# A three-stage transformer kernel: setup work moved between engines, the end of self-attention reordered, feed-forward weights turned one group at a time

## The reference, cut to what matters

```python
x = x + xattn(ctx_1024, ctx_1024, layernorm(x), lens, lens, ...)   # 32 batches, 64 queries, 1601 keys, 16 heads of 16
x = x + attn(layernorm(x), ...)          # causal self-attention with position bias, projection, a layernorm of its own
x = x + ffn(layernorm(x), ...)           # quantised feed-forward, inner size 768

# ffn:
x = act_qdq(x); up = act_qdq(x @ dq(w_up).T); gate = act_qdq(x @ dq(w_gate).T)
gate = act_qdq(gate * fixed_qdq(sigmoid(gate)))
return act_qdq(gate * up) @ dq(w_down).T
```

## Time and profile before

| | |
|---|---|
| median of 3 executions | 1581.92 us (1581.59 to 1583.39) |
| profiled execution | 1582.63 us, of which the span of instructions is 1580.8 us |
| PE busy | 1389.4 us (88%) |
| DVE busy | 1061.8 us (67%) |
| ACT busy | 881.5 us (56%) |
| POOL busy | 789.2 us (50%) |
| cross-attention, setup and batch -1 | 0 to 92.7 us |
| cross-attention, batches 0 to 31 | to about 1215 us |
| self-attention | to 1392.3 us |
| feed-forward | to 1580.8 us |

### The profile page before, as it was taken

One profiled execution on the slowest core, in us unless ns is written; L12 is line 12 of the kernel. 1 busy time (PEld: TensorE's weight loads), 2 busy tenths in 40 slices (PEclk: granted clock), 3 DMA queues, 4 the chain that ended last, 5 costly groups with the idle time before them and its releaser, 6 DMA issues. The chain is left out here.

```text
span 1580.8 us, 55267 instructions
## 1 busy us (share of the span) xinstructions
PE 1389.4 (88%) x24351; PEld 989.7 (63%) x24351; DVE 1061.8 (67%) x1681; ACT 881.5 (56%) x1195; POOL 789.2 (50%) x560
## 2 busy tenths in 40 slices
PE   4679999999999999999999999999997687459408
PEld 2457777777777777777777777777775355324107
DVE  7756666666666666666666666666664867785984
ACT  1445655665656565665556565656565565425742
POOL 4566555555655555555555555555530798420000
PEclk9899999999999999999999999999999898769859
DMA  4564444544444444444444444444421421010001
GB/s 150 145 137 137 107 107 110 128 120 120 117 127 132 107 107 116 121 124 122 114 136 121 107 107 120 124 124 114 117 65 53 131 54 27 1 41 0 1 0 54
DMA packets 90495, 155.97 MB, mean 99 GB/s; under 512 B 16704, under 2 KB 55496, under 8 KB 90256
## 3 DMA queue, kind: packets, MB, share of 16 engines
q1 hardware_dynamic: 88256, 150.92, 36.6%
q10 hardware_dynamic: 2000, 1.51, 0.4%
HBM read 60.95 MB, written 2.20 MB: 40 GB/s over the span
## 5 line engine op out<-in xcount | busy, mean ns | idle before, releaser
L645 DVE TENSOR_REDUCE MXP<-W_PS 128x1 f32<-128x512 f32 x768 | 510.7, 688 | 339.8 <-PE W_PS L456 338.7
L540 ACT ACTIVATE PR<-S_PS 128x1024 f32<-128x1024 f32 (+1 forms) x416 | 409.0, 1030 | 144.8 <-PE S_PS L404 142.8
L350 POOL TENSOR_TENSOR K_HI<-K,MCOL 128x512 f16<-128x512 f32 (+1 forms) x224 | 215.2, 961 | 282.8 <-ACT K L548 282.8
L356 POOL TENSOR_TENSOR CTX_LO<-CTX,CTX_HI 128x3202 f16<-128x3202 f32 x32 | 194.1, 6067 | 190.9 <-DVE CTX_HI L623 190.9
L456 PE MATMUL W_PS<-STK,QS 105*128 105x512 f16 (+1 forms) x1024 | 279.9, 336 | 10.1 <-POOL STK L377 6.1
L548 ACT ACTIVATE K<-W_PS,BK 128x512 f32<-128x512 f32 (+1 forms) x256 | 148.3, 593 | 175.9 <-PE W_PS L430 157.1
L404 PE MATMUL S_PS<-QS,STK 105*128 105x128 f16 (+1 forms) x3328 | 238.9, 220 | 4.2 <-ACT PR L540 2.9
L352 POOL TENSOR_TENSOR K_LO<-K,K_HI 128x512 f16<-128x512 f32 (+1 forms) x224 | 232.0, 1036 | 17.6
L404 PEld LDWEIGHTS S_PS<-QS,STK 105*128 105x128 f16 (+1 forms) x3328 | 210.4, 99 | 48.2 <-ACT PR L540 3.8
L439 PE MATMUL W_PS<-WV_HI,CTX_HI 128*128 128x256 f16 (+1 forms) x832 | 228.0, 274 | 2.8 <-ACT K L548 2.6
L439 PE MATMUL W_PS<-WV_HI,CTX_LO 128*128 128x256 f16 (+1 forms) x832 | 227.4, 273 | 0.0
(11 more groups left out here) (243 smaller groups left out, 1593.5 us busy)
## 6 DMA issues: line engine op xcount, KB each, us to landing
CTX<-in_ctx_t SPq DMA_DIRECT2D x64, 800.5 KB, 5.8
STK<-K_HI SPq DMA_DIRECT2D x256, 128.0 KB, 2.5
STK<-K_HI SPq DMA_DIRECT2D x256, 72.1 KB, 2.1
STK<-K_LO SPq DMA_DIRECT2D x128, 128.0 KB, 2.6
STK<-K_LO SPq DMA_DIRECT2D x128, 72.1 KB, 2.1
QSTK<-STK SPq DMA_DIRECT2D x12, 192.0 KB
SQS<-QK_HI SPq DMA_DIRECT2D x32, 64.0 KB, 2.2
X<-in_x SPq DMA_DIRECT2D x1, 1536.0 KB, 16.3
```

What stands on the lines that cost most here:

```text
L350: pool.tensor_tensor(K_HI[:, m, lo:hi], k32, zero, ALU.add).then_inc(k_hi, 1)
L356: pool.tensor_tensor(CTX_LO[:, u, :, :], CTX[:, :, :], CTX_HI[:, u, :, :], ALU.subtract).then_inc(ctx_lo, 1)
L540: nc.scalar.activation(PR[0:m, (NT * b + i) % PR_RING, :], S_PS[par][0:m, :], ACT.Exp).then_inc(p_sb, 1)
L645: dve.tensor_reduce(MXP[:, j, at:at + 1], bank[:, :], AX.X, ALU.max).then_inc(mx_done, 1)
```

## The change

It has three parts.

1. **Setup of cross-attention.** The high parts of the weights, of batch 0's context and of query chunk 0 are made by ACT; DVE makes the low parts, batch 0's `CTX_LO` among them, in two halves. For batches 0 and 1 ACT makes `K_HI` from the PSUM bank beside `K32`, and POOL only `K_LO`. The loads are issued in another order. ACT issues 6 of the 12 transfers of batch 0's first half stack (`SK`). The late layernorm root (`SQ`), rows (`RW`) and mask (`QM`) become steps of `FIRST`, whose order changes. The ones of `STK[1]` are copied from `STK[0]` by a DMA. `QSTK`'s memset moves ahead of batch 0 on POOL. PE runs 28 matmuls whose result nobody reads.
2. **End of self-attention.** `centred`, `normal_again`, the group products and `maximum(0)` are placed differently; the transposes `XT 0` move behind the pipeline.
3. **Feed-forward.** The weights are turned one group ahead of each of gate chunks 12 to 21; the first eight gate and up chunks are taken in another order; the first gate integer tensor is made by DVE, and ACT makes four up tensors first and then alternates.

```diff
+START = [("K", 0), ("QH", 0), ("K", 1), ("K", 2), ("K", 3), ("K", 4), ("K", 5), ("K", 6)]
 FIRST = [
...
+    ("V", 0), ("SK", 2), ("SK", 3), ("SQ", 1), ("V", 1), ("RW", 1), ("QM", 1), ("V", 2), ("V", 3), ("TN", 1),
+    ("CH", 0), ("RW", 2), ("V", 4), ("QS", 0), ("MX", 0), ("MX", 1), ("QY", 1), ("MX", 2), ("MX", 3), ("TN", 2),
+    ("RW", 3), ("MX", 4), ("MX", 5), ("V", 5), ("MX", 6), ("MX", 7), ("QY", 2), ("MX", 8), ("MX", 9), ("TN", 3),
+    ("MX", 10), ("MX", 11), ("V", 6), ("MX", 12), ("MX", 13), ("QY", 3), ("MX", 14), ("MX", 15), ("K", 0), ("MX", 16),
+    ("MX", 17), ("K", 1), ("MX", 18), ("MX", 19), ("K", 2), ("MX", 20), ("MX", 21), ("K", 3), ("MX", 22), ("MX", 23),
+    ("K", 4), ("MX", 24), ("MX", 25), ("MT", 0), ("K", 5), ("K", 6),
 ]
+EARLY_K = 2
...
+    def stack_rows(eng, u, c, lo, hi, done):
+        rows = slice(32 * c, 32 * c + 32)
+        for q, part in enumerate((K_HI, K_LO, K_HI)):
+            eng.dma_start(STK[u][32 * q:32 * q + 32, c::4, lo:hi], part[rows, :, lo:hi]).then_inc(done[c], 16)
...
         sp.wait_ge(q_rest, 16 * 13)
+        sp.dma_start(STK_MEM[1][ROW_M:ROW_MASK, :], STK_MEM[0][ROW_M:ROW_MASK, :]).then_inc(stk_m, 16)
...
         def ctx_low(n, u):
-            pool.wait_ge(ctx_hi, n + 1)
+            pool.wait_ge(ctx_hi, n + 2)
+            if n == 1:
+                pool.wait_ge(qs_ready, 2)
...
+        pool.wait_ge(k_lo, 2 * PER["K"])
+        pool.memset(QSTK[ROW_M:ROW_MASK, :, CH:ROWS].bitcast(F32), 0.0).then_inc(q_zero, 1)
...
-        pool.memset(STK_MEM[1][ROW_M:ROW_MASK, :].bitcast(F32), ones).then_inc(constant, 1)
...
+        pe.wait_ge(constant, 1)
+        idle(18)
+        pe.wait_ge(in_cst, 16 * 4)
         turn(0)
+        idle(10)
         query(0)
...
+                        for s, m in enumerate(range(ms.start, ms.stop)):
+                            last = nc.scalar.activation(K_HI[:, m, lo:hi], bank[:, s * LAST:s * LAST + hi - lo], ACT.Identity,
+                                                        bias=BK[:, m:m + 1], scale=1 / W_SCALE)
+                        last.then_inc(k_hi, 1)
...
+                elif kind == "SK":
+                    act.wait_ge(k_lo, 4)
+                    stack_rows(act, 0, i, 0, HALF, stk_a)
...
-ENDING = [("XT", 1, 0), ("XT", 1, 1), ("XT", 2, 0), ("XT", 2, 1), ("XT", 3, 0), ("XT", 3, 1)]
+ENDING = [("XT", 0, 0), ("XT", 0, 1), ("XT", 1, 0), ("XT", 1, 1), ("XT", 2, 0), ("XT", 2, 1), ("XT", 3, 0), ("XT", 3, 1)]
-WEIGHTED = {13: (0, 4), 14: (4, 8), 17: (8, 13)}
+WEIGHTED = {13: [(0, 4)], 14: [(4, 8)], 17: [(8, 10), (10, 13)]}
...
+            if s == 17:
+                act.wait_ge(sm["chain"], 2 * CHAIN)
+                centred(range(8, 10))
...
-            if s == 16:
-                act.wait_ge(sm["chain"], 2 * CHAIN)
-                centred(range(8, 13))
-                normal_again(range(0, 4))
             if s == 17:
-                normal_again(range(4, 8))
+                centred(range(10, 13))
+                normal_again(range(0, 8))
...
             if s == 18:
-                maximum(0)
                 add_weighted(2, 8, 13)
         dve.wait_ge(sm["y_stat"], 16 + 13)
         scale_rows(2)
+        maximum(0)
         add_rows(range(*GROUPS[2]))
...
-TURN = {8: 0, 16: 1}
+TURN = {12: (0, 0), 13: (0, 1), 14: (0, 2), 15: (0, 3),
+        16: (1, 0), 17: (1, 1), 18: (1, 2), 19: (1, 3), 20: (1, 4), 21: (1, 5)}
+UP_EARLY = 4
...
+    def place(i):
+        return (i % 2, i // 2) if i < 8 else (i // 4, i % 4)
...
+        for f in range(UP_EARLY):
+            up_integer(f)
         act.wait_ge(sm["sc"], 4 * SSTEPS)
-        for f in range(FT):
+        for f in range(1, FT):
             nc.scalar.activation(GI[:, f, :], G[:, f, :], ACT.Copy, scale=INV[:, 3:4]).then_inc(sm["g2i"], 1)
+            if UP_EARLY + f - 1 < FT:
+                up_integer(UP_EARLY + f - 1)
...
+        dve.tensor_scalar(GI[:, 0, :], G[:, 0, :], INV[:, 3:4], None, ALU.mult).then_inc(sm["giv"], 1)
```

More of the change, by code:

```diff
@@ L278, in stack @@
             lo, hi = (0, HALF) if half == 0 else (HALF, LK)
-            done = stk_a if half == 0 else stk_b
             if half == 0:
                 need(sp, s_ps, NT * (n - 1))
+                if n == 0:
+                    sp.wait_ge(mask_out, 16)
             sp.wait_ge(k_lo, PER["K"] * n + (4 if half == 0 else 7))
             if half == 0:
-                sp.dma_start(STK[u][ROW_MASK:ROW_MASK + 1, :, :],
-                             dram["kmask"][bass.ds(n, 1), :].rearrange("a (o t) -> a o t", o=1).broadcast_to([1, PAIRS, LK]))\
-                    .then_inc(stk_m, 16)
+                mask_row(sp, n, u)
             for c in range(4):
-                rows = slice(32 * c, 32 * c + 32)
-                for q, part in enumerate((K_HI, K_LO, K_HI)):
-                    sp.dma_start(STK[u][32 * q:32 * q + 32, c::4, lo:hi], part[rows, :, lo:hi]).then_inc(done[c], 16)
+                if ("SK", c) not in FIRST or n or half:
+                    stack_rows(sp, u, c, lo, hi, stk_a if half == 0 else stk_b)
         def query_stack(lo, hi, done):
@@ L341, in k_low @@
             k32 = K32[:, (PER["K"] * n + i) % K_RING, 0:size].rearrange("p (m t) -> p m t", t=hi - lo)
+            if n < EARLY_K:
+                pool.wait_ge(k_hi, PER["K"] * n + i + 1)
+                pool.tensor_tensor(K_LO[:, m, lo:hi], k32, K_HI[:, m, lo:hi], ALU.subtract).then_inc(k_lo, 1)
+                return
             pool.wait_ge(k_32, k_written(n, i))
@@ L376, in _ @@
         pool.wait_ge(constant, V_ONES[1])
-        pool.memset(STK_MEM[1][ROW_M:ROW_MASK, :].bitcast(F32), ones).then_inc(constant, 1)
[L378 to L383, removed]
+        for b in range(B):
             body(b)
@@ L493, in query, with idle @@
             last.then_inc(q_ps, 1)
-        pe.wait_ge(in_cst, 16)
+        def idle(count):
+            for _ in range(count):
+                pe.matmul(W_PS[2][:, 0:2 * P], MCOL[:, 0:SQ].bitcast(F16), MCOL[:, :].bitcast(F16), start=True, stop=True)
+        pe.wait_ge(constant, 1)
+        idle(18)
+        pe.wait_ge(in_cst, 16 * 4)
         turn(0)
+        idle(10)
         query(0)
@@ L513, in _, with w_high @@
     def _(act):
+        for dst, src in ((LENI[:, :], dram["lens"].broadcast_to([P, B])), (LENPI[:, :], dram["lens"].rearrange("a b -> b a")),
+                         (BQ[:, :], dram["bq"])):
+            act.dma_start(dst, src).then_inc(in_cst, 16)
         act.dma_start(CST[:, :], dram["cst"]).then_inc(in_cst, 16)
[L515 to L521, removed]
-        act.dma_start(W_RAW[2], dram["wv_t"].rearrange("(k p) n -> p k n", p=P)).then_inc(in_wv, 16)
+        act.dma_start(BK[:, :], dram["bk"]).then_inc(in_b, 16)
+        def w_high(raw, hi, landed):
+            act.wait_ge(landed, 16)
+            nc.scalar.activation(hi, raw, ACT.Copy, scale=W_SCALE).then_inc(w_hi, 1)
         def o_copy(b):
@@ L1275, in _ @@
                     .then_inc(sm["xb"], 1)
-            if s in WEIGHTED:
-                lo, hi = WEIGHTED[s]
+            for lo, hi in WEIGHTED.get(s, []):
                 pool.wait_ge(sm["xz"], hi)
```

200 lines of the change are left out of this document (116 added, 84 removed), and 7 rows, old and new, of tables (BESIDE, FIRST).

## The result

In the comparison made after the prediction the changed kernel took 1555.13 us (median of 4 runs, 1553.25 to 1560.07) against 1582.19 (4 runs, 1581.59 to 1583.39) of the kernel before: a ratio of 0.9833, 95% interval 0.9809 to 0.9857. The forecast was 1556.0. In a second comparison it took 1558.53 (5 runs, 1555.06 to 1560.46) against 1582.15, ratio 0.9853, 0.9840 to 0.9866. So it gains 23 to 27 us by the two medians, and its runs scatter more (7 and 5 us) than those of before (2 and 4). That the first median lies only 0.9 us from the forecast is partly luck: the second lies 2.5 above it. Four parts were predicted, and each can be read at its own place.

What follows compares the result with a forecast made beforehand. PE bounds the batches without a gap, so time can be won only at the two ends. 9.5 + 3.9 + 8.5 + 4.0 = 25.9 us takes the median from 1581.92 to 1556.0; range for 8 in 10: 1547 to 1566.

Steps and rivals of the forecast that it cites:

- the setup: Cross-attention up to batch 1's first MX: start moves from 101.22 to 91.7 us, 9.5 us won, between -3 and 13.
- self-attention: End of self-attention: DVE's addition starts 5.1 us earlier, when POOL is done; a maximum returns behind it; net 3.9 us, 3 to 5.
- the gate chunks: Feed-forward: turning weights by groups brings the first up chunk to 1439.3 from 1447.78; 8.5 us, 8 to 10.5.
- the integers: Feed-forward: DVE makes the first gate tensor, so its product starts at 1508.2 instead of 1512.24; 4.0 us.
- Setup, first MX: Start of cross-attention: the first row-maximum matmul comes at about 43.5, 10.1 us earlier than 53.60.
- the six issues cost these 3.9 us in full: Setup: ACT's six transfer issues, at 0.6 to 0.65 us each, delay its root by 3.9 us, to 34.4.
- long done with the statistics: Setup: DVE has finished the layernorm statistics well before ACT's root at 34.4, so the root waits only for ACT.
- Batch -1: Cross-attention before batch 0: query rounds take 8.7 us (7.17 before); batch 0's scores at about 83, 9.7 us earlier.
- if each of the eight went through its own engine, 2.1 us. I take this one, hidden: Before batch 1's first MX: eight rows of 25.6 KB copy over separate DMA engines in 2.1 us, costing nothing.
- the first rival: Setup gives its gain back (17%): ones copy or competing transfers delay batch 1's MX to 98 to 104; about 1565 us.
- The stand of 5.5 us: Gate chunks: PE, done with chunk 13, waits 5.5 us for DVE before the third group of transposes.
- A slower rhythm of the batches: Rival (4%): batches 0 to 31 settle in another rhythm; at 1 us more per batch the kernel takes 1587 us.

Runs made afterwards that it cites:

- the parts: Four kernels, each the kernel before with one part alone (setup, self-attention, gate chunks, integers); their gains sum to 25.8 us.
- after: The changed kernel in the first comparison, against the kernel before: median 1555.13 us, ratio 0.9833; its profiled execution took 1560.07 us.
- sk_on_sync: The changed kernel, but SP issues all twelve transfers of batch 0's first half stack and ACT none: 1556.89 us, ratio 0.9827.
- again: The changed kernel once more, unchanged, in a second comparison against the kernel before: 1558.53 us, ratio 0.9853.
- low_first: The changed kernel, but DVE takes the up weight's low parts before pending gate maxima and the down weight is turned two chunks later: 1549.60 us, ratio 0.9801.
- before: The kernel before the change, nothing altered: median 1582.19 us in the first comparison.
- ones_cut: The changed kernel, but the copy of the ones goes in 64 pieces of 3.2 KB instead of 8 of 25.6 KB: 1557.15 us, ratio 0.9833.
- ones_on_act: The changed kernel, but ACT instead of SP issues the copy of the ones, ahead of batch 0's scores: 1556.10 us, ratio 0.9838.
- split_q: The changed kernel, but SP issues the query stack's last three chunks one by one as each is ready: 1555.35 us, ratio 0.9832.

## Why the prediction was right

**The sum.** 25.9 was forecast; 27.1 and 23.6 were measured, 25.8 by the parts. In the places: 8.7 for the setup as a mean (forecast 9.5; 6.5 between the two profiled executions, by B), 5.2 for self-attention (3.9), 8.6 for the gate chunks (8.5), 4.0 for the integers (4.0), 26.5 together. Two errors of about a microsecond, setup too high and self-attention too low, cancel in it. In the two profiled executions it is 6.5 + 5.2 + 8.6 + 4.0 = 24.3, less 1.7 us that `after` took longer from B to the first weighted addition (154.03 against 152.34); that leaves 22.6, and the spans differ by 22.5.

**Setup, first MX.** Forecast 43.5, came at 42.6. The mask operation, `CTX_LO` on DVE (3.56, forecast 3.8) and the keys came as costed. The step "the six issues cost these 3.9 us in full" was too large: DVE was not "long done with the statistics" but ended them at 30.9, so about 2 us remain (2.1 in `sk_on_sync` against `again`).

**Batch -1.** Round 8.7 forecast, 8.58 at full clock; batch 0's scores 83 forecast, 83.7 measured.

**The stop before batch 1.** SP went on at 85.65 as forecast (85.8). The step "if each of the eight went through its own engine, 2.1 us. I take this one, hidden" failed. The copy takes 4.1 us by the estimate above, and what is issued behind it waits; the MX came 8.2 us after SP went on, where 5.9 were forecast (85.8 to 91.7; the terms written out there add up to 5.6). That is the first rival's mechanism at a price of 2.1 us instead of 6 to 12, and executions whose query rounds ran at full rate win more than that back (MX at 90.23): the setup came near its forecast with this term wrong.

**Self-attention.** The mechanism was right, and the term mis-sized: POOL's first product began as soon as the first two tiles were there, and both had ended 4.9 us after DVE's last step of the chain (1359.34 to 1364.28), where the forecast's 1370.3 is 6.2 behind the same step of the kernel before (1364.11). That is 1.3 us sooner than the forecast had it, and DVE follows at once: 5.2 instead of 3.9.

**Gate.** The stand of 5.5 us came as 5.93, the half rate behind it for about two chunks, and the first up chunk at 42.4 after the first gate chunk (8.5 off 50.94 is 42.4; the list of signs said 40 to 42). What I did not ask is whether DVE's order could be changed: `low_first` shows 8.5 us lying there.

**Rivals.** A slower rhythm of the batches did not come: from the first MX of batch 1 to B it is 1092.7 us in `after` and 1091.8 in `before`, 0.03 us a batch, and the other kernels lie between 1091.4 and 1093.2 with either code. "More than I count" is the one that single executions touch, by the clock.

## What to carry to other kernels

Cost each part at its own place, between two landmarks whose distance repeats from execution to execution, and let the whole time only confirm the sum. When a producer is cut into pieces, give the consumer's engine the same cut: the pieces must stand ahead of that engine's backlog of work that nobody waits for. Before a memset is replaced by a copy over few partitions, price the copy by its own rate and ask what is queued behind it.

## What the runs showed of the hardware

A copy of 205 KB over eight partitions ran at 38 to 45 GB/s in 64 pieces (`ones_cut`) and took 4.1 us per piece in eight (50 GB/s, an estimate), where the transfers of the query stack, 32 partitions each, move at 184 to 206 together (most microseconds from 73 to 84 of `again`). Behind it next to nothing else moved for 2 to 3 us, whichever queue had issued it (88 to 91 us in `again`, 85 to 87 in `ones_on_act`), and the issuing of one transfer took 3.2 to 3.5 us.

The granted clock at one place differs between executions of one kernel: 0.50 or 1.00 in the last batch's scores, 0.60 to 0.96 from 40 to 50 us. At the end of self-attention, 0.50 instead of 1.00 for 8 us went with a stretch 1.5 us longer (`split_q`). In nine timed executions of the changed kernel the mean granted clock goes with the time: 0.946 to 0.951 for 1558.5 to 1560.5 us, 0.953 to 0.956 for 1553.3 to 1555.9.
